# Linear attention inside a four-layer kernel: the output projection in three passes of rounded high and low parts

## The chip, the cores and the metric

The kernel runs on one core of a Trainium2 chip. The metric is the device time of one execution in microseconds, the median of three runs. TensorE multiplies matrices; VectorE (DVE), ScalarE (ACT) and GpSimd (POOL) work on tiles; SyncE (SP) and GpSimd issue transfers. Each engine runs its own instruction stream in order, and streams meet only at semaphores: a `wait_ge` stops everything behind it on its engine.

## The reference

Four layers in a row, each adding its result to `x` of shape (4, 256, 64, 64): window attention, linear attention, channel attention, dynamic convolution, each on a group norm of `x`. The change is in the second layer. Cut to what matters:

```python
ms = jnp.concatenate([qkv, agg], axis=1)          # 64 heads of 8 channels, from two scales
q, k, v = ...                                     # q and k through relu, v with a column of ones
kv = jnp.einsum('bgnd,bgne->bgde', k, v)
out = jnp.einsum('bgnd,bgde->bgne', q, kv)
out = out[..., :-1] / (out[..., -1:] + EPS)       # the division
x = x + _conv2d(out, w_proj)                      # 512 channels in, 256 out: the projection and the residual
```

## The kernel before

The whole program is a sequence of blocks: group norm, window attention, group norm, qkv projection, grouped convolution, `linear_attention`, group norm, channel attention, group norm, dynamic convolution. A block begins when the one before has ended on all engines. `linear_attention` takes 2792 to 3548 us of the profiled execution.

It works on 4 images. For each image the 512 channels are ST = 4 tiles of 128, and the 4096 pixels are NPC = 8 chunks of PC = 512. First comes the sum over keys and values (`turn` transposes a chunk of keys and of values on TensorE, ScalarE and VectorE copy them out of PSUM, `accumulate` multiplies them into `pkv`), 32 times for each image. Then, for each of NI = 32 pairs (chunk, tile) of an image, numbered i, comes one step of the main loop: `ratio` multiplies queries by the summed keys and values (numerators and denominators, 8 records in the profile), `divide` on VectorE adds EPS, takes the reciprocal and multiplies twice, `back` transposes the result on TensorE into the one buffer `att_bank`, ScalarE copies it to `att` in SBUF, and `project` multiplies it by the weights `wp` into `pp`, two matmuls of 512 columns that accumulate over the four tiles of a chunk. After the fourth tile VectorE adds `pp` to the residual `xr` (`add`), and GpSimd stores the chunk (`pool.dma_start` of `x_out`) and loads a later one into the same buffer (`load`).

The order on TensorE is written out by hand (the loop at the end of its function). In step i of image b it does: `ratio(b, i)`, `turn` and `accumulate` for image b + 1 (if there is one), `project(b, i - 1)`, `back(b, i)`. So the projection lags one step behind its own transpose. At i = 0 of a later image the order is `turn`, `accumulate`, `project(b - 1, 31)`, `ratio(b, 0)`, `back(b, 0)`. In the last image (b = 3) there is no `turn` and no `accumulate`. The first image's sum of keys and values has a loop of its own ahead of the main loop.

ScalarE's order in a step: `copy_keys`, then at eight of the 32 steps (`CLIP_AT`) `clip_queries`, which waits for queries that SyncE loads, then the copy of `att`. VectorE's: `divide`, `copy_values`, and `add` at every fourth step. GpSimd does nothing here but transfers: two loads ahead, then for each chunk a store once it is added, and a load into the same buffer, for which it waits until the store has landed. All matmuls are in float32, each of which the profile shows as two records. Buffers that matter: `att` two, `attp` two, `att_bank` one, `pp` one, `xr` two.

Of the kernel before, what the change touches and what calls it, by code (L numbers as in the profile page):

```python
# [6 lines left out]
ACT = mybir.ActivationFunctionType  # L7
AX = mybir.AxisListType
F32 = mybir.dt.float32
F32R = mybir.dt.float32r  # L10

B, C, HH, WW = 4, 256, 64, 64
NPX = HH * WW
PART = 128
HALVES = C // PART
# [966 lines left out]
ST = SCALES * HEADS1 // TG  # L982
# [3 lines left out]
def linear_attention(nc, scales, x_in, x_out, w_proj_t, head_mask, ident_in):  # L986
# [3 lines left out]
    with ctx:  # L990
        sb = lambda n, s, dt=F32: ctx.enter_context(nc.sbuf_tensor(f"d_{n}", s, dt))
        pb = lambda n, s: ctx.enter_context(nc.psum_tensor(f"d_{n}", s, F32))
        sem = lambda n: nc.alloc_semaphore(name=f"d_{n}")
        TPS = ST // SCALES
        PC = 512
        NPC = NPX // PC
        SUB = PC // PART
        SPB = SUB // 2
        NI = NPC * ST
# [6 lines left out]
        kvp = [sb(f"kvp{u}", [PART, SUB, 2 * PART + 1]) for u in range(NKV)]  # L1006
        kvm = [sb(f"kvm{u}", [PART, ST, ONE]) for u in range(2)]
        wp = sb("wp", [PART, ST, C])
        hm = sb("hm", [PART, PART])
        ident = sb("ident", [PART, PART])  # L1010
        den = [sb(f"den{u}", [PART, SUB, TG]) for u in range(2)]
        attp = [sb(f"attp{u}", [PART, SUB, PART]) for u in range(2)]
        att = [sb(f"att{u}", [PART, PC]) for u in range(2)]
        xr = [sb(f"xr{u}", [PART, HALVES, PC]) for u in range(2)]
        keys_turned = pb("keys_turned", [PART, SUB, PART])
        values_turned = pb("values_turned", [PART, SUB, PART])
# [2 lines left out]
        att_bank = pb("att_bank", [PART, PC])  # L1019
        pp = pb("pp", [PART, HALVES, PC])  # L1020
        ratios = ratio_banks[:, :, 0:SPB * ONE].rearrange("p b (s n) -> p b s n", n=ONE)
        consts_in = sem("consts_in")
        wp_in = sem("wp_in")
# [10 lines left out]
        den_steps = sem("den_steps")  # L1034
        attended = sem("attended")
        turned_back = sem("turned_back")
        att_copied = sem("att_copied")
        projected = sem("projected")
        added = sem("added")
        x_loaded = [sem(f"x_loaded{u}") for u in range(2)]  # L1040
# [2 lines left out]
        QPT = NPX // PC  # L1043
# [56 lines left out]
        @block.gpsimd  # L1100
        def _(pool):
            def of_chunk(t, b, c):
                return t[b:b + 1, :, c * PC:(c + 1) * PC].rearrange("b (h p) n -> p (b h) n", p=PART)

            def load(k):
                if k >= 2:

                    pool.wait_ge(stored[k % 2], k // 2 * 16)
                pool.dma_start(xr[k % 2][:], of_chunk(x_in, *divmod(k, NPC))).then_inc(x_loaded[k % 2], 16)

            load(0)
            load(1)
            for k in range(B * NPC):
                pool.wait_ge(added, (k + 1) * HALVES)
                pool.dma_start(of_chunk(x_out, *divmod(k, NPC)), xr[k % 2][:]).then_inc(stored[k % 2], 16)
                if k + 2 < B * NPC:
                    load(k + 2)
            for u in range(2):
                pool.wait_ge(stored[u], B * NPC // 2 * 16)

        @block.tensor
        def _(pe):
            pe.wait_ge(consts_in, 32)
            pe.wait_ge(ones_ready, NKV)

            def turn(j):

                g, k = divmod(j, QPH)
                if k == 0:
                    pe.wait_ge(kv_in[g % NH], (g // NH + 1) * (2 * len(HALF_RUNS[g % 2]) * 16))  # L1130
                if j:

                    pe.wait_ge(keys_copied, j)
                    pe.wait_ge(values_copied, j)
                for bank, buf in ((keys_turned, kt), (values_turned, vt)):
                    for e in range(SUB):
                        last = nc.tensor.transpose(bank[:, e, :], buf[g % NH][:, k * PC + e * PART:k * PC + (e + 1) * PART], ident[:])
                last.then_inc(turned, 1)

            def accumulate(j):  # L1140
                tile, k = divmod(j, QPT)
                pe.wait_ge(keys_copied, j + 1)
                pe.wait_ge(values_copied, j + 1)
                if k == 0 and tile:

                    pe.wait_ge(sums_masked, tile * 2)
                for e in range(SUB):
                    last = nc.tensor.matmul(pkv[:, 0:PART + 1], lhsT=kvp[j % NKV][:, e, 0:PART],
                                            rhs=kvp[j % NKV][:, e, PART:2 * PART + 1],
                                            start=k == 0 and e == 0, stop=k == QPT - 1 and e == SUB - 1)  # L1150
                last.then_inc(summed, 1)

            def ratio(b, i):
                c, st = divmod(i, ST)
                if c % (NPC // 2) == 0:
                    pe.wait_ge(q_positive, b * (2 * ST) + (2 * c // NPC) * ST + st + 1)
                if c == 0:
                    pe.wait_ge(sums_masked, (b * ST + st + 1) * 2)
                if b or i:

                    pe.wait_ge(attended, b * NI + i)
                for s in range(SUB):
                    queries = qt[:, st, c * PC + s * PART:c * PC + (s + 1) * PART]
                    last = nc.tensor.matmul(ratios[:, s // SPB, s % SPB, :], lhsT=queries, rhs=kvm[b % 2][:, st],
                                            start=True, stop=True)
                last.then_inc(rated, 1)

            def back(b, i):
                pe.wait_ge(attended, b * NI + i + 1)
                if b or i:  # L1170

                    pe.wait_ge(att_copied, b * NI + i)
                for s in range(SUB):
                    last = nc.tensor.transpose(att_bank[:, s * PART:(s + 1) * PART], attp[i % 2][:, s], ident[:])
                last.then_inc(turned_back, 1)

            def project(b, i):
                c, st = divmod(i, ST)
                pe.wait_ge(att_copied, b * NI + i + 1)
                if st == 0 and (b or c):  # L1180

                    pe.wait_ge(added, (b * NPC + c) * HALVES)
                for m in range(HALVES):
                    last = nc.tensor.matmul(pp[:, m, :], lhsT=wp[:, st, m * PART:(m + 1) * PART],
                                            rhs=att[i % 2][:], start=st == 0, stop=st == ST - 1)
                last.then_inc(projected, 1)

            for j in range(NQ):
                turn(j)
                if j:  # L1190
                    accumulate(j - 1)
            pe.wait_ge(wp_in, 16)
            for b in range(B):
                for i in range(NI):
                    if i or not b:
                        ratio(b, i)
                    j = (b + 1) * NQ + i
                    if b + 1 < B:
                        turn(j)
                    if b + 1 < B or i == 0:  # L1200
                        accumulate(j - 1)
                    if i:
                        project(b, i - 1)
                    elif b:
                        project(b - 1, NI - 1)
                        ratio(b, 0)
                    back(b, i)
            project(B - 1, NI - 1)

        @block.scalar  # L1210
        def _(act):
            def copy_keys(j):
                act.wait_ge(turned, j + 1)
                if j >= NKV:

                    act.wait_ge(summed, j - NKV + 1)
                nc.scalar.activation(kvp[j % NKV][:, :, 0:PART], keys_turned[:], ACT.Relu).then_inc(keys_copied, 1)

            def clip_queries(b, v, st):
                act.wait_ge(q_in[v][st // 2], (b + 1) * (2 * len(HALF_RUNS[v]) * 16))  # L1220
                part = slice(v * (NPX // 2), (v + 1) * (NPX // 2))
                nc.scalar.activation(qt[:, st, part], qt[:, st, part], ACT.Relu).then_inc(q_positive, 1)

            for j in range(NQ):
                copy_keys(j)
            for st in range(ST):
                clip_queries(0, 0, st)
            for b in range(B):
                for i in range(NI):
                    if b + 1 < B:  # L1230
                        copy_keys((b + 1) * NQ + i)
                    if i in CLIP_AT:
                        clip_queries(b, 1, CLIP_AT[i])
                    if b + 1 < B and i - NI // 2 in CLIP_AT:
                        clip_queries(b + 1, 0, CLIP_AT[i - NI // 2])
                    act.wait_ge(turned_back, b * NI + i + 1)
                    if b or i >= 2:

                        act.wait_ge(projected, b * NI + i - 1)
                    nc.scalar.activation(att[i % 2][:], att_bank[:], ACT.Copy).then_inc(att_copied, 1)  # L1240

        @block.vector
# [958 lines left out]
```

## Time and profile before

| | us |
|---|---|
| median of 3 runs | 8986.69 |
| lowest, highest | 8982.88, 8989.02 |
| the profiled execution | 8987.96 |
| its span in the trace | 8986.0 |

| engine | busy, us | share of the span |
|---|---|---|
| TensorE, matmuls | 8007.1 | 89% |
| VectorE | 5706.7 | 64% |
| GpSimd | 4530.7 | 50% |
| ScalarE | 3532.7 | 39% |

All times in the views are microseconds from the start of the span unless marked ns. A matmul row of a timeline is a run of equal instructions: its start, how long it lasts, the engine, the line, output <- inputs, shapes, and xN records; a bracket behind it is the idle time of the engine just before it and what ended it. Matmuls are pipelined, so a run's duration reaches beyond the start of the next run; the distance from start to start is what a run costs. The granted clock is TensorE's clock as a share of 2.4 GHz; 0.5 is 1.2 GHz.

### The profile page before, as it was taken

To read this page: it belongs to the slowest core of one execution; us is meant where nothing else is said; L and a number is where in the kernel's file an instruction comes from. 1 tells how busy PE (TensorE), PEld (TensorE's weight loads), DVE (VectorE), ACT (ScalarE), POOL (GpSimd) and SP (SyncE) were. 2 spreads that over 40 slices of the span, in tenths; PEclk is the share of its full clock that TensorE was granted. 3 is DMA by queue.
4 is the path that set the end of the run, shared out by engine and by line. 5 is a ranking of instruction groups with operands and counts; after the bars stand their busy time and mean duration, and the time that the engine had idled before them with its cause. 6 is when DMAs were issued, how large, how long until landed. Compare 5 with 4: busy or idle time off the path is not lost. (4 is left out here: it accounts for less than half of the span.)

```text
span 8986.0 us, 157002 instructions
## 1 busy us (share of the span) xinstructions
PE 8007.1 (89%) x55850; PEld 6800.4 (76%) x55850; DVE 5706.7 (64%) x9055; ACT 3532.7 (39%) x6841; POOL 4530.7 (50%) x2037
## 2 busy tenths in 40 slices
PE   3999995889997897499999999999999999919999
PEld 3777774679996675388888888888888888817777
DVE  4555555334442444698989889898988889841110
ACT  3545444323332332355544444454454445520000
POOL 2554543013331001288777778787877788811111
PEclk9999997999998999799999999999999999959999
DMA  5111113865555554300000000000000000071111
GB/s 208 54 56 62 53 62 150 298 191 144 147 141 171 205 200 139 131 6 18 18 18 18 13 18 6 18 18 18 18 13 18 6 18 18 8 222 61 63 62 55
DMA packets 439682, 706.22 MB, mean 79 GB/s; under 512 B 273781, under 2 KB 288629, under 8 KB 429622
## 3 DMA queue, kind: packets, MB, share of 16 engines
q1 hardware_dynamic: 400438, 521.76, 18.4%
q0 software_dynamic: 38656, 176.79, 5.3%
q8 instruction: 349, 5.72, 0.3%
q14 instruction: 239, 1.96, 0.1%
HBM read 425.22 MB, written 273.22 MB: 78 GB/s over the span
## 5 line engine op out<-in xcount | busy, mean ns | idle before, releaser
L1740 POOL TENSOR_TENSOR e_ev<-e_se,e_v 128x2048 f32<-128x2048 f32 (+1 forms) x896 | 3311.7, 3713 | 915.4 <-ACT e_se L1706 914.7
L1706 ACT ACTIVATE e_se<-e_stage 128x512 f32<-128x512 f32 x3136 | 1878.4, 599 | 2082.4 <-PE e_stage L1580 2052.2
L1830 DVE SCALAR_TENSOR_TENSOR e_stage<-e_k,e_rl,e_qp 128x512 f32<-128x512 f32 x3136 | 2308.1, 748 | 319.5 <-ACT e_se L1706 277.3
L1587 PE MATMUL e_pv_sum<-e_ident,e_ev 128*128 128x128 f32 x12544 | 1873.5, 273 | 34.9 <-issue 34.5
L1587 PE MATMUL e_pe_sum<-e_ident,e_se 128*128 128x128 f32 x12544 | 1878.8, 272 | 0.1
L1587 PEld LDWEIGHTS e_pe_sum<-e_ident,e_se 128*128 128x128 f32 x12544 | 1556.6, 140 | 227.4 <-issue 1.8
L1587 PEld LDWEIGHTS e_pv_sum<-e_ident,e_ev 128*128 128x128 f32 x12544 | 1488.1, 141 | 266.3 <-issue 212.3
L1580 PE MATMUL e_stage<-e_top,e_minus 128*128 128x512 f32 x3136 | 1510.0, 481 | 46.8 <-DVE e_stage L1830 44.9
L377 POOL TENSOR_TENSOR a_pr<-a_pr,a_rden 128x480 f32<-128x480 f32 x512 | 494.6, 987 | 672.1 <-DVE a_rden L601 672.1
L863 POOL DMA_DIRECT2D agg<-c_ot x384 | 329.1, 862 | 871.7 <-DVE c_ot L922 760.0
L1580 PEld LDWEIGHTS e_stage<-e_top,e_minus 128*128 128x128 f32 x3136 | 597.6, 191 | 96.4 <-DVE e_stage L1830 72.8
L1569 PE MATMUL e_pj<-e_xb,e_wt 128*128 128x385 f32 (+5 forms) x1280 | 570.1, 529 | 73.8 <-ACT e_v L1680 60.9
L898 PE MATMUL c_pa<-c_x_high,c_w_high 128*128 128x320 f32 x1920 | 603.1, 314 | 34.2 <-DVE c_w_low L962 34.2
L564 ACT ACTIVATE a_pr<-a_ps,a_nmax 128x240 f32<-128x240 f32 x1024 | 458.8, 459 | 419.6 <-DVE a_nmax L595 419.6
L898 PE MATMUL c_pa<-c_x_high,c_w_low 128*128 128x320 f32 x1920 | 604.8, 315 | 0.0
L898 PE MATMUL c_pa<-c_x_low,c_w_high 128*128 128x320 f32 x1920 | 603.0, 314 | 0.0
L1806 DVE SCALAR_TENSOR_TENSOR e_ext<-e_near,e_rl,e_ext 128x512 f32<-128x512 f32 x768 | 576.2, 750 | 0.9
L595 DVE TENSOR_REDUCE a_nmax<-a_ps 128x2 f32<-128x480 f32 x512 | 312.8, 653 | 338.8 <-PE a_ps L459 331.6
L1787 DVE TENSOR_REDUCE e_near<-e_pair 128x192 f32<-128x768 f32 (+2 forms) x512 | 517.5, 1011 | 0.6
L2135 DVE TENSOR_TENSOR f_xr<-f_pc,f_xr 128x512 f32<-128x512 f32 x64 | 44.2, 691 | 743.2 <-PE f_pc L2048 743.2
L2002 POOL TENSOR_TENSOR f_x_low<-f_xb,f_x_high 128x1400 fp32r<-128x1400 f32 x32 | 106.3, 3327 | 800.6 <-ACT f_x_high L2078 800.6
L2048 PE MATMUL f_pc<-f_x_high,f_w_high 128*128 128x512 f32 x1152 | 467.9, 406 | 22.3 <-POOL f_x_low L2002 22.3
(150 smaller groups left out, 12078.9 us busy)
## 6 DMA issues: line engine op xcount, KB each, us to landing
xn<-n_xnp POOLq DMA_DIRECT2D x32, 2450.0 KB, 15.0
qkv<-b_ot SPq DMA_DIRECT2D x120, 512.0 KB, 5.9
c_xt<-qkv SPq DMA_DIRECT2D x384, 160.0 KB, 3.8
agg<-c_ot POOLq DMA_DIRECT2D x384, 160.0 KB, 2.5
n_xt<-x SPq DMA_DIRECT2D x24, 2048.0 KB, 11.9
a_xb<-xn SPq DMA_DIRECT2D x32, 840.0 KB, 6.8
e_xb<-xn SPq DMA_DIRECT2D x16, 1540.0 KB, 6.9
f_xb<-xn SPq DMA_DIRECT2D x32, 700.0 KB, 6.2
```

The source lines that it names most:

```text
L377: nc.gpsimd.tensor_tensor(w, w, by, ALU.mult).then_inc(normalised, 1)
L564: last = nc.scalar.activation(pr[P % BUF][:, i, e, :], ps[:, 2 * s + i, e * NK:(e + 1) * NK], ACT.Exp, bias=nmax[P % BUF][:, i, e:e + 1], ...
L898: last = nc.tensor.matmul(pa[:, u, b, 0:NBLK * WW].rearrange("p (k c) -> p k c", c=WW), lhsT=w[u][:, dx].rearrange("p o y -> p (o y)"), rh ...
L1569: last = nc.tensor.matmul(out, lhsT=wt[:, w, g, (h % 2) * PART:(h % 2 + 1) * PART], rhs=rhs, start=g == 0, stop=g == HALVES - 1)
L1580: nc.tensor.matmul(stage[:, bank_of(t, j), :], lhsT=minus[:], rhs=top[h][:, u * TPX:(u + 1) * TPX], start=False, stop=True, skip_group_che ...
L1587: last = nc.tensor.matmul(acc[:, c * PART:(c + 1) * PART], lhsT=src[:, c * PART:(c + 1) * PART], rhs=ident[:], is_transpose=True, start=j ...
L1706: nc.scalar.activation(se[(t * K2 + o) % NSE][:, i], stage[:, bank_of(t, j), :], ACT.Exp)\
L1740: nc.gpsimd.tensor_tensor(split(ev[(t * NG2 + g) % NEV][:, 0:size]), split(se[(t * K2 + o) % NSE][:, i:i + size]), window(v[h], h, u, o, i ...
L1787: nc.vector.tensor_reduce(to, pairs, AX.XY, op).then_inc(near_step, 1)
L1806: nc.vector.scalar_tensor_tensor(rows(ext[:]), win, r[:, o:o + 1], rows(ext[:]), ALU.add, op)\
L1830: nc.vector.scalar_tensor_tensor(rows(stage[:, bank_of(t, j), :]), win, rl[:, h, o:o + 1], rows(qp[:]), ALU.add, ALU.mult).then_inc(multip ...
L2048: last = nc.tensor.matmul(pc[:, u, m].rearrange("p (r c) -> p r c", c=WW), lhsT=w[:, g, t, m * PART:(m + 1) * PART], rhs=x[:, g, dy:dy + R ...
```

## The change

The projection's operands are split. ScalarE rounds the weights `wp` to `wp_high` (float32r) once, after its ninth key copy, and GpSimd computes `wp_low = wp - wp_high`. In each step ScalarE copies `att_bank` twice, to `att_high` (rounded) and to `att`, and GpSimd computes `att_low = att - att_high`. `project` is then three accumulating passes for each half: high by high, low by high, high by low. It waits for GpSimd's subtraction instead of ScalarE's copy.

Two orders change with it. On TensorE, `back(b, i)` now stands before `project(b, i - 1)` (the order at i = 0 of a later image stays). On GpSimd, the store of chunk k - 1 comes at the last tile of chunk k, behind its split, and the load of chunk k at the second tile of chunk k.

```diff
+        wp_high = sb("wp_high", [PART, ST, C], F32R)
+        wp_low = sb("wp_low", [PART, ST, C], F32R)
...
+        att_high = [sb(f"att_high{u}", [PART, PC], F32R) for u in range(2)]
+        att_low = [sb(f"att_low{u}", [PART, PC], F32R) for u in range(2)]
...
+            def split(b, i):
+
+                j = b * NI + i
+                pool.wait_ge(att_copied, (j + 1) * 2)
+                if j >= 2:
+
+                    pool.wait_ge(projected, j - 1)
+                nc.gpsimd.tensor_tensor(att_low[j % 2][:], att[j % 2][:], att_high[j % 2][:].bitcast(F32), ALU.subtract)\
+                    .then_inc(att_split, 1)
+
+            def exchange(k):
+                pool.wait_ge(added, (k + 1) * HALVES)
+                pool.dma_start(of_chunk(x_out, *divmod(k, NPC)), xr[k % 2][:]).then_inc(stored[k % 2], 16)
+
             load(0)
             load(1)
+            flat = lambda t: t[:].rearrange("p s o -> p (s o)")
+            pool.wait_ge(wp_split, 1)
+            nc.gpsimd.tensor_tensor(flat(wp_low), flat(wp), flat(wp_high).bitcast(F32), ALU.subtract).then_inc(wp_split, 1)
             for k in range(B * NPC):
-                pool.wait_ge(added, (k + 1) * HALVES)
-                pool.dma_start(of_chunk(x_out, *divmod(k, NPC)), xr[k % 2][:]).then_inc(stored[k % 2], 16)
-                if k + 2 < B * NPC:
-                    load(k + 2)
+                for st in range(ST):
+                    split(k // NPC, k % NPC * ST + st)
+                    if st == ST - 1 and k:
+                        exchange(k - 1)
+                    if st == 1 and k >= 2:
+                        load(k)
+            exchange(B * NPC - 1)
...
-                    pe.wait_ge(att_copied, b * NI + i)
+                    pe.wait_ge(att_copied, (b * NI + i) * 2)
...
             def project(b, i):
                 c, st = divmod(i, ST)
-                pe.wait_ge(att_copied, b * NI + i + 1)
+                pe.wait_ge(att_split, b * NI + i + 1)
...
                 for m in range(HALVES):
-                    last = nc.tensor.matmul(pp[:, m, :], lhsT=wp[:, st, m * PART:(m + 1) * PART],
-                                            rhs=att[i % 2][:], start=st == 0, stop=st == ST - 1)
+                    for p, (w, a) in enumerate(((wp_high, att_high), (wp_low, att_high), (wp_high, att_low))):
+                        last = nc.tensor.matmul(pp[:, m, :], lhsT=w[:, st, m * PART:(m + 1) * PART], rhs=a[i % 2][:],
+                                                start=st == 0 and p == 0, stop=st == ST - 1 and p == 2)
...
-            pe.wait_ge(wp_in, 16)
+            pe.wait_ge(wp_split, 2)
...
-                    if i:
-                        project(b, i - 1)
-                    elif b:
+                    if i == 0 and b:
                         project(b - 1, NI - 1)
                         ratio(b, 0)
                     back(b, i)
+                    if i:
+                        project(b, i - 1)
...
             for j in range(NQ):
                 copy_keys(j)
+                if j == QPT:
+                    act.wait_ge(wp_in, 16)
+                    nc.scalar.activation(wp_high[:], wp[:], ACT.Copy).then_inc(wp_split, 1)
...
+                    nc.scalar.activation(att_high[i % 2][:], att_bank[:], ACT.Copy).then_inc(att_copied, 1)
                     nc.scalar.activation(att[i % 2][:], att_bank[:], ACT.Copy).then_inc(att_copied, 1)
```

## Rows read from the trace of the kernel before

**Rows 1.** The page, part 1: busy time, share and instructions of each engine.
```profile
PE 8007.1 (89%) x55850; PEld 6800.4 (76%) x55850; DVE 5706.7 (64%) x9055; ACT 3532.7 (39%) x6841; POOL 4530.7 (50%) x2037
```
**Rows 2.** Stretches: PE, PEld, DVE, ACT, POOL busy (instructions), granted clock, DMA share, GB/s.
```profile
2904.00:3010.00 106.00, 72.03 (x417) 57.47 (x418) 31.97 (x75) 29.62 (x34) 2.86 (x4) 0.78 0.55 209
3120.00:3230.00 110.00, 106.55 (x677) 84.09 (x677) 51.87 (x119) 36.03 (x49) 7.68 (x11) 0.97 0.59 199
3441.00:3544.00 103.00, 102.71 (x491) 63.06 (x490) 56.54 (x138) 25.36 (x35) 10.01 (x14) 1.00 0.32 104
```
**Rows 3.** Timeline of one step of the first three images, from ratio to ratio.
```profile
3202.82 1.15 PE L1164 MATMUL d_ratio_banks<-d_kvm,d_qt 128*128 128x144 f32 x8
...
3204.85 0.76 DVE L1278 TENSOR_TENSOR d_attp<-d_ratio_banks,d_den 128x256 f32<-128x256 f32 x2
...
3205.57 1.88 PE L1184 MATMUL d_pp<-d_att,d_wp 128*128 128x512 f32 x4
...
3207.29 0.60 PE L1174 MATMUL d_att_bank<-d_ident,d_attp 128*128 128x128 f32 x4
...
3207.73 1.15 PE L1164 MATMUL d_ratio_banks<-d_kvm,d_qt 128*128 128x144 f32 x8
3207.93 0.60 ACT L1240 ACTIVATE d_att<-d_att_bank 128x512 f32<-128x512 f32 x1 [2.45 <-PE d_att_bank L1174]
```
**Rows 4.** Timeline of one step of the last image, from back to back.
```profile
3483.05 0.66 PE L1174 MATMUL d_att_bank<-d_ident,d_attp 128*128 128x128 f32 x4
...
3483.54 1.15 PE L1164 MATMUL d_ratio_banks<-d_kvm,d_qt 128*128 128x144 f32 x8
...
3484.52 1.88 PE L1184 MATMUL d_pp<-d_att,d_wp 128*128 128x512 f32 x4
...
3485.57 0.76 DVE L1278 TENSOR_TENSOR d_attp<-d_ratio_banks,d_den 128x256 f32<-128x256 f32 x2
...
3486.38 0.66 PE L1174 MATMUL d_att_bank<-d_ident,d_attp 128*128 128x128 f32 x4
```
**Rows 5.** Timeline of the qkv projection: first and last of 28 passes in a row.
```profile
1749.65 0.39 PE L746 MATMUL b_pq<-b_x_high,b_w_low 128*128 128x512 f32 x1
...
1755.77 0.39 PE L746 MATMUL b_pq<-b_x_high,b_w_low 128*128 128x512 f32 x1
```
**Rows 6.** Timeline at the last change of image: ratio, then back.
```profile
3436.66 1.15 PE L1164 MATMUL d_ratio_banks<-d_kvm,d_qt 128*128 128x144 f32 x8
...
3439.71 0.66 PE L1174 MATMUL d_att_bank<-d_ident,d_attp 128*128 128x128 f32 x4 [1.91 <-DVE d_attp L1278]
```
**Rows 7.** Groups by shape, GpSimd: busy us, mean ns, idle before and its releaser.
```profile
L377 POOL TENSOR_TENSOR a_pr<-a_pr,a_rden 128x480 f32<-128x480 f32 x512 | 494.6, 987 | 672.1 <-DVE a_rden L601 672.1
...
L2002 POOL TENSOR_TENSOR f_x_low<-f_xb,f_x_high 128x1400 fp32r<-128x1400 f32 x32 | 106.3, 3327 | 800.6 <-ACT f_x_high L2078 800.6
```
**Rows 8.** Timeline at the stage's end: the last back and the last project.
```profile
3543.05 0.66 PE L1174 MATMUL d_att_bank<-d_ident,d_attp 128*128 128x128 f32 x4
...
3544.40 1.98 PE L1184 MATMUL d_pp<-d_att,d_wp 128*128 128x512 f32 x4 [0.69 <-ACT d_att L1240]
```
**Rows 9.** The tile d_wp: its DMA (duration ns, first and last start us), landing.
```profile
L1090 SPq DMA_DIRECT2D d_wp<-in_L_w_proj_t x1: 916/916/916, 2828.8 to 2828.8; - x1
...
DMA to landing us min/median/max: 15.7/15.7/15.7
```
**Rows 10.** Timeline of ScalarE: the first clips of queries.
```profile
2906.07 3.71 ACT L1222 ACTIVATE d_qt<-d_qt 128x2048 f32<-128x2048 f32 x2 [12.75 <-DMA d_qt<-qkv]
```
**Rows 11.** Waits: who waited for whom, us in total, times, longest.
```profile
POOL d_xr L1109 <- DMA x<-d_xr: 175.0, 30, 8.0
```
**Rows 12.** Waits of TensorE from 2904 to 3445 us, same columns.
```profile
PE d_pp L1184 <- ACT d_att L1240: 21.4, 3, 14.8
```
**Rows 13.** Stretches behind the second and last change of image (columns as rows 2).
```profile
3280.00:3285.00 5.00, 5.00 (x29) 4.86 (x28) 2.22 (x5) 1.20 (x2) 0.00 (x0) 0.66 0.63 194
...
3440.00:3445.00 5.00, 5.00 (x30) 3.48 (x29) 1.78 (x6) 1.19 (x2) 0.00 (x0) 1.00 0.63 195
```

More of the change, by code:

```diff
@@ L1036, in linear_attention @@
         turned_back = sem("turned_back")
+        wp_split = sem("wp_split")
         att_copied = sem("att_copied")
+        att_split = sem("att_split")
         projected = sem("projected")
```

## Prediction

> **What bounds the kernel now.** I read the page first, for the busy shares (TensorE 89% of the 8986 us [rows 1]), and then the busy time by stretch, because the page's chain of work that ended last reaches back only into the last stage (from about 8045 us) and says nothing of the stage that is changed. The linear attention runs from 2792 to 3548 us. The stretches show two different regimes in it [rows 2]: while a next image still has keys and values to sum (b = 0 to 2), TensorE is busy 106.55 of 110 us; in the last image (b = 3, from 3441 us) 102.71 of 103 us. Both look bound by TensorE. The timelines show that only the first is.
>
> In a step of the first three images [rows 3], `ratio` starts at 3202.82, `turn` and `accumulate` follow, `project` starts at 3205.57, `back` at 3207.29 and the next `ratio` at 3207.73: 4.91 us with no gap, of which `project` holds 1.72 and `back` 0.44. The divide chain of VectorE (add, reciprocal, two multiplies) ends at 3204.85 + 0.76 = 3205.61, which is 2.79 us after `ratio`; `back`, which needs it, comes 4.47 us after. So VectorE is hidden there, with 1.7 us of cover, and that cover is `project`.
>
> In a step of the last image [rows 4] there is no `turn` and no `accumulate`. `back` to `ratio` is 0.49, `ratio` to `project` 0.98, `project` to `back` 1.86: 3.33 us. `back` starts 0.05 us after the multiplies end (3485.57 + 0.76 = 3486.33) and 2.84 us after `ratio`. Without a wait `project` would have held 1.72, so the chain of VectorE already sets this step, by 0.14 us, although the busy share says 100%: `project` lies over the chain and hides nearly all of it.
>
> **The change part by part.**
>
> *Passes.* Before, the two matmuls of a step appear as four records 0.43 us apart, 1.72 us. After, there are six of one rounded pass each. The qkv projection runs the same form (128x512, contiguous, high and low parts): from 1749.65 to 1755.77 us are 27 intervals, 0.227 us each [rows 5]. Six cost 1.36 us, 0.36 less than before. The Trainium skill ("TensorE: Matmul & The Clock Gate", Back-to-back issue gap) gives N/2.4 + 2.5 ns for an isolated pass at the higher clock, 216 ns for 512 columns. By it six passes would be 1.30 us and my sum 8 us lower; the row is of the same form, so the row decides.
>
> *Order.* `back(i)` moves ahead of `project(i-1)`. This is the largest term. `back(i)` now stands directly behind `accumulate` (or, in the last image, directly behind `ratio`) and waits for the divide of its own step. Queued behind that wait are `project(i-1)`, and behind it the next `ratio`, which starts the next divide. So the step becomes a loop through VectorE: 2.84 (`ratio` to `back`) + 0.49 (`back` after a wait) + 1.36 (`project`) = 4.69 us, in all four images.
> First three images: TensorE would be ready for `back` 2.75 us after `ratio` [rows 3], so 0.09 us of the chain shows, and the step goes from 4.91 to 4.69, a gain of 0.22. I count 87 such steps (93, less six in the stretch up to 2975 us that waits for queries anyway): -19 us. Three changes of image keep their order and gain only the passes, 3 x 0.36 = -1 us.
> Last image: 3.33 becomes 4.69, since `turn` and `accumulate` are missing and the cover of `project` is gone. 31 x 1.36 = +42 us.
>
> *The residual add.* Every fourth step VectorE adds two tiles after the last projection of a chunk. Before, `back` lay between that projection and `ratio`. After, `ratio` follows directly, and the add (about 1.3 us) delays the next divide. The change of image already has this order: `ratio` at 3436.66, `back` at 3439.71, 3.05 us against 2.84 [rows 6]. So +0.21 for 20 steps in the first three images (+4 us) and 7 in the last (+1.5 us).
>
> *Splits.* ScalarE makes two copies of about 0.6 us, starting 0.64 us after `back` [rows 3]; GpSimd then subtracts 128x512. No row has that size: by 480 columns in 987 ns it is 1.05 us, by 1400 in 3327 ns 1.22 us [rows 7]; I take 1.2, the rate of the row that is also a subtraction into rounded form. The low part is ready about 0.64 + 1.2 + 1.2 = 3.1 us after `back(i)` with the semaphores; `project(i)` comes after the next `back`, 4.69 + 0.49 = 5.2 us after. Two microseconds of slack: nothing, and if the slack were gone each microsecond beyond it would cost one per step. Where ScalarE clips queries between (1.9 us, four times per half image) the slack is just used up. At the change of image `project(31)` comes 3.6 us after its `back`: still covered. At the very end it is not: `back` at 3543.05, `project` at 3544.40 [rows 8]; now about 3.15 us instead of 1.35, less 0.4 for shorter passes: +1.4 us.
>
> *Weights' split.* ScalarE waits for the projection's weights behind its ninth key copy, and all later key copies stand behind that. The weights' transfer is issued at 2828.8 and takes 15.7 us to land [rows 9], so ScalarE may stand still until about 2845 us, and `turn` with it. But the opening is paced by transfers, and the first `ratio` waits for a clip of queries that ScalarE starts at 2906.07 after 12.75 us of idle time for their DMA [rows 10]. Whatever is late by less than that is hidden. Cost 0; with the cover gone it is the stop less that idle time, 3 us.
>
> *GpSimd's transfers.* `load(k)` and `exchange(k-1)` with 0.7 us of issuing each now stand between subtractions. Before, GpSimd waited 175.0 us in 30 times, 8.0 at most, for a store to land before loading [rows 11]; now two steps (9.4 us) lie between, so it waits little and no subtraction is late. A chunk's load has three steps to land. Cost 0. The first store and reload, 1 MB, move behind the longest wait for queries (below); at the 209 GB/s of that stretch [rows 2] this is 5 us of traffic, partly on other queues: between 0 and -5, I take -3 us.
>
> *Waits for queries.* Where a clip waits for its queries, the copies of `att` stand behind it and TensorE waits: 21.4 us in 3 times, 14.8 the longest, so some 3.3 each for the other two [rows 12]. They end when a DMA lands, not when TensorE is ready. The some 6.5 steps between issue and clip give nothing for the two short ones (2 x 6.5 x 0.22 = +3), and restarting now passes through two copies and a subtraction: +0.7 each of three, +2.
>
> *The clock.* In the last image TensorE will idle 1.7 us of each 4.69. At a change of image it idles 1.91 [rows 6]; after the second of the three the granted clock of the next 5 us was 0.66, after the last 1.00 [rows 13]. 0.66 over 5 us is 3.4 us at 1.2 GHz and the rest at 2.4. Some of the 32 new gaps will be followed by such a dip. TensorE works 60% of the new step, so a dip takes 3.4 x 0.6 / 2 = 1.0 us, and a little more where it stretches the chain: 1.1. Ends: none (0) and all (+35). The rows have one dip in two; these gaps are a little shorter, and I take seven in 32, +8 us.
>
> **Sum**, against the profiled execution's 8987.96 us: first three images -19 - 1 + 4 + 3 + 2 - 3 = -14; last image 42 + 1.5 + 8 = +51.5; end +1.4. Together +39, 9027; the median is 1.3 below the profiled run: 9026 us.
>
> **The rivals.**
> (a) The clock stays low for half of the last image. For it: a gap in every step, where today there is one in 32, and one of the two shown was followed by a dip. Against: a dip ends by itself within 5 us in the rows. At 1.2 GHz `ratio` (+1.0), `back` (+0.5) and `project` (+1.3) stretch, +2.8 a step; 15 steps: +43 in place of +8, 9061 us.
> (b) GpSimd slows VectorE. Divide chain and add run beside a GpSimd subtraction for the first time here. Against it: the subtraction runs from 1.9 to 3.1 us after `back`, the divide starts at 3.04, so they hardly meet. With 0.2 us more in each of 118 looped steps: +24, 9050 us. The Trainium skill ("GPSIMD Engine Reference", Key points) says that GpSimd shares its SBUF interfaces with VectorE, with contention where VectorE has two SBUF inputs or a 2-port mode; the divide and the add each read PSUM for one operand.
> (c) The other side: the query waits go. The first three images last 536 us where 96 steps of 4.91 are 471, so 65 us are waits for queries and what follows them. If the later stores and loads let the queries land in time, these go. It ends faster once more than 39 us of the 65 go beyond what I count; with 60, 8966 us. Against: the loads moved are 1 MB in the stretch where the long waits are, worth 5 us.
> (d) The rounded passes are not one pass each, and take 0.43 us: 6 x 0.43 is 1.2 more than I count, 128 times, about 9180 us. The qkv rows speak against it.
>
> **How the numbers follow.** Forecast 0.69, (a) 0.14, (b) 0.07, (c) 0.05, (d) 0.01, and 0.04 for the gain and loss terms just cancelling. A difference of 0.2% (18 us) is about what a measurement of this kernel can tell from no change. The forecast's own spread is from 9012 (no dips, full transfer gain) to 9045. The range takes in (a), (b) and part of the cancelling: 9004 to 9062. Faster 0.04, same 0.07, slower 0.89.
>
> **What would show it.** The profile after should have `back` waiting on VectorE's multiplies in nearly every step: about 0.1 us in the first three images, 1.7 us in the last (some 50 to 60 us in total); steps of 4.69 us in both, the last image lasting about 150 us instead of 107; projection records 0.227 us apart; GpSimd's subtraction near 1.2 us with no TensorE wait behind it. I am wrong if the last image's steps stay near 3.3 us, if `project` waits for GpSimd, or if TensorE's query waits change by over 10 us.

## The result: 0.4% slower, lost in the last image

| | before | changed |
|---|---|---|
| median, us (5 runs each) | 8987.23 | 9025.25 |
| lowest to highest | 8982.88 to 8989.02 | 9022.46 to 9032.19 |
| profiled execution / its span | 8987.96 / 8986.0 | 9023.35 / 9021.4 |

The ratio is 1.0039, interval 1.0028 to 1.0050. The busy shares of the page hardly tell the two kernels apart; TensorE has less to do (8007.1 us in [rows 1]) and the time is longer:

```profile
PE 7984.4 (89%) x56106; PEld 6863.7 (76%) x56106; DVE 5703.0 (63%) x9055; ACT 3595.9 (40%) x6970; POOL 4693.3 (52%) x2166
```

A step of the first three images after the change, in the timeline (columns as in [rows 3]):

```profile
3196.97 1.14 PE L1190 MATMUL d_ratio_banks<-d_kvm,d_qt 128*128 128x144 f32 x8
...
3198.99 0.76 DVE L1309 TENSOR_TENSOR d_attp<-d_ratio_banks,d_den 128x256 f32<-128x256 f32 x2
...
3199.80 0.66 PE L1200 MATMUL d_att_bank<-d_ident,d_attp 128*128 128x128 f32 x4
3200.22 0.47 PE L1211 MATMUL d_pp<-d_att_high,d_wp_high 128*128 128x512 f32 x1
...
3201.66 1.27 POOL L1124 TENSOR_TENSOR d_att_low<-d_att,d_att_high 128x512 fp32r<-128x512 f32 x1 [3.44 <-ACT d_att L1271]
3201.68 1.14 PE L1190 MATMUL d_ratio_banks<-d_kvm,d_qt 128*128 128x144 f32 x8
```

`back` starts 0.05 us after the multiplies end (3198.99 + 0.76), 2.83 after `ratio`, and the step is 4.71 us instead of 4.91. `project` has gone behind `back` and takes 1.46 us to the next `ratio`. A step of the last image, to compare with [rows 4]:

```profile
3490.05 0.66 PE L1200 MATMUL d_att_bank<-d_ident,d_attp 128*128 128x128 f32 x4 [1.69 <-DVE d_attp L1309]
3490.47 0.47 PE L1211 MATMUL d_pp<-d_att_high,d_wp_high 128*128 128x512 f32 x1
...
3491.92 1.26 POOL L1124 TENSOR_TENSOR d_att_low<-d_att,d_att_high 128x512 fp32r<-128x512 f32 x1 [4.25 <-ACT d_att L1271]
3491.94 1.14 PE L1190 MATMUL d_ratio_banks<-d_kvm,d_qt 128*128 128x144 f32 x8
...
3493.96 0.75 DVE L1309 TENSOR_TENSOR d_attp<-d_ratio_banks,d_den 128x256 f32<-128x256 f32 x2
3494.77 0.66 PE L1200 MATMUL d_att_bank<-d_ident,d_attp 128*128 128x128 f32 x4 [1.69 <-DVE d_attp L1309]
```

The same loop, and now 1.69 us of idle TensorE in it: 4.72 us instead of 3.33. Who TensorE waited for in the whole stage (us in total, times, longest):

```profile
PE d_att_bank L1200 <- DVE d_attp L1309: 61.7, 35, 2.0
...
PE d_keys_turned L1163 <- ACT d_kvp L1244: 22.8, 2, 13.0
PE d_att_bank L1200 <- ACT d_att L1271: 17.9, 3, 12.9
...
PE d_pp L1211 <- POOL d_att_low L1124: 2.8, 5, 1.1
```

The wait for VectorE has 35 entries: the 31 steps of the last image and the four points where it stood before. GpSimd is waited for 2.8 us in all. By starts of rows, the 35.4 us between the spans lie here:

| stretch | before | changed | difference | forecast |
|---|---|---|---|---|
| span's start to first `ratio` | 2908.1 | 2910.0 | +1.9 | 0 |
| to the last change of image (`back` of [rows 6]) | 531.6 | 511.7 | -19.9 | -14 |
| to the last `back` | 103.3 | 155.7 | +52.3 | +51.5 |
| to the span's end | 5442.9 | 5444.0 | +1.1 | +1.4 |

### The profile page after: what moved, and what is told of

The parts are those of the page before. It is cut to its first block and busy times, and to the rows that moved or that the text cites. A ratio compares the mean times of both kernels' runs of the same rounds, so it can differ in the third digit from the quotient of the medians.

```text
span 9021.4 us, 157898 instructions
## 1 busy us (share of the span) xinstructions
PE 7984.4 (89%) x56106; PEld 6863.7 (76%) x56106; DVE 5703.0 (63%) x9055; ACT 3595.9 (40%) x6970; POOL 4693.3 (52%) x2166
```

## The experiments

Theory 1 is that of the prediction: the divide on VectorE closes a loop with TensorE, and the position of `project` decides whether it is covered. Theory 2 is the rival that the eye falls on, since it is what the change added: the copies and GpSimd's subtraction set the pace, or GpSimd slows VectorE. Each result is beside runs of the kernel before on the same chip.

### The old order with everything else changed

```diff
-                    if i == 0 and b:
-                        project(b - 1, NI - 1)
-                        ratio(b, 0)
-                    back(b, i)
-                    if i:
-                        project(b, i - 1)
+                    if i:
+                        project(b, i - 1)
+                    elif b:
+                        project(b - 1, NI - 1)
+                        ratio(b, 0)
+                    back(b, i)
```

> The changed kernel with TensorE's old order (project(i-1) before back(i)), all else as changed. Theory 1 (the loop through VectorE's divide sets the changed steps): the wait at back goes, but project now stands 3.2 us too near its own transpose, since two copies and the subtraction take 3.2 us after back. First three images: project is ready to start 3.2 us after back, so nearly no wait, step 4.6 us (-0.12 each). Last image: project waits for GpSimd some 1.7 us in every step, step 3.2 + 1.4 = 4.6 us, about as bad as now. Time about 9010 us. Theory 2 (the new order costs nothing, the loss in the last image is the longer chain of copies and subtraction): undoing the order changes neither regime by more than 0.1 us a step, 9015 to 9030 us, and the wait stands at project in both kernels.

Measured 9003.2 us beside 8986.1, ratio 1.0018 (1.0008 to 1.0027). Two steps of its last image, and its waits of TensorE from 3410 us on:

```profile
3462.38 0.50 PE L1211 MATMUL d_pp<-d_att_high,d_wp_high 128*128 128x512 f32 x1 [1.54 <-POOL d_att_low L1124]
...
3463.87 0.60 PE L1200 MATMUL d_att_bank<-d_ident,d_attp 128*128 128x128 f32 x4
...
3467.00 0.50 PE L1211 MATMUL d_pp<-d_att_high,d_wp_high 128*128 128x512 f32 x1 [1.55 <-POOL d_att_low L1124]
```
```profile
PE d_pp L1211 <- POOL d_att_low L1124: 51.0, 33, 2.5
```

The wait moves from `back` to `project`, and from VectorE to GpSimd; the step is 4.62 us in both regimes, as theory 1 worked out. So theory 2 is false of the changed order but true of the old one: with a lag of one step and the old order, the low part comes 1.5 us late in the last image. The new order changes one exposed chain for another that is 0.1 us longer in each step, 0.3 where an add follows, and that the clock falls in (below). Together this costs: with the old order the kernel is 17 us slower than the kernel before, with the new one 38, and the two intervals do not meet. In the traces 10.6 us of the difference lie in the last image (145.0 us from first to last `back` against 155.7) and 9.5 in the first three. So the old order alone would have saved about half of the loss, and not all of it.

### The order alone, in the kernel before

The edit above in reverse, made in the kernel before: float32 passes, no split.

> The kernel before with only TensorE's order changed (back(i) before project(i-1)); no split, no rounded passes, GpSimd as before. Theory 1: the loop of the divide is 2.84 + 0.49 + 1.72 = 5.05 us in all four images. First three images +0.14 each step and +0.2 at every add: +17 us. Last image 3.33 to 5.05 in 31 steps, +53, with the adds and clock dips +64. Time about 9067 us (+80), back waiting on VectorE 1.7 us a step in the last image. Theory 2: order alone costs nothing, 8987 us.

Measured 9057.1 us beside 8986.1, ratio 1.0074 (1.0057 to 1.0090): 71 us against 80 forecast and 0 for theory 2. Its last image:

```profile
3461.75 0.66 PE L1174 MATMUL d_att_bank<-d_ident,d_attp 128*128 128x128 f32 x4 [1.70 <-DVE d_attp L1278]
3462.25 1.88 PE L1184 MATMUL d_pp<-d_att,d_wp 128*128 128x512 f32 x4
...
3463.97 1.14 PE L1164 MATMUL d_ratio_banks<-d_kvm,d_qt 128*128 128x144 f32 x8
...
3466.80 0.66 PE L1174 MATMUL d_att_bank<-d_ident,d_attp 128*128 128x128 f32 x4 [1.70 <-DVE d_attp L1278]
```

5.05 us a step with no GpSimd work in it. The order alone makes the wait. The sum was nearly met, its parts less so. In the trace the last image is 53.0 us longer where I had 64: no dip of the clock came (I had some 9 us of them), and one step of the 31 holds no projection and stays 3.33. The first three images are 10.3 us longer where I had 17. Another 7 us lie before and behind the four images, where the change has no part.

### GpSimd's subtraction twice

```diff
+        again = sb("again", [PART, PC], F32R)
...
+                if j:
+                    pool.wait_ge(att_split, j * 2)
+                nc.gpsimd.tensor_tensor(again[:], att[j % 2][:], att_high[j % 2][:].bitcast(F32), ALU.subtract).then_inc(att_split, 1)
                 nc.gpsimd.tensor_tensor(att_low[j % 2][:], att[j % 2][:], att_high[j % 2][:].bitcast(F32), ALU.subtract)\
                     .then_inc(att_split, 1)
...
-                pe.wait_ge(att_split, b * NI + i + 1)
+                pe.wait_ge(att_split, (b * NI + i + 1) * 2)
```

> The changed kernel with GpSimd's subtraction done twice in each step (the first into a spare tile), which doubles its 1.27 us. Theory 1: the low part is then ready 4.5 us after back where it is needed 5.2 us after; nothing in a usual step. At the three changes of image and at the end it comes 1 us late each, and where clips of queries stand between, some tenths: 9028 to 9038 us. Theory 2 (GpSimd's work sets the step, or slows VectorE): +1.3 us in each of 31 to 118 steps, 9065 to 9180 us.

Measured 9041.7 us beside 8986.1 (four runs, 9030.6 to 9052.7), ratio 1.0064 (1.0048 to 1.0081); the profiled execution took about 9031. A step of its last image and TensorE's wait for GpSimd from 3427 us on:

```profile
3465.13 1.26 POOL L1127 TENSOR_TENSOR d_again<-d_att,d_att_high 128x512 fp32r<-128x512 f32 x1 [2.88 <-ACT d_att L1275]
...
3466.32 0.23 DVE L1303 TENSOR_SCALAR d_den<-d_ratio_banks 128x64 f32<-128x64 f32 x1 [3.12 <-PE d_ratio_banks L1194]
3466.36 1.26 POOL L1128 TENSOR_TENSOR d_att_low<-d_att,d_att_high 128x512 fp32r<-128x512 f32 x1
3466.58 0.55 DVE L1306 RECIPROCAL d_den<-d_den 128x64 f32<-128x64 f32 x1
3467.17 0.76 DVE L1313 TENSOR_TENSOR d_attp<-d_ratio_banks,d_den 128x256 f32<-128x256 f32 x2
...
3467.98 0.66 PE L1204 MATMUL d_att_bank<-d_ident,d_attp 128*128 128x128 f32 x4 [1.70 <-DVE d_attp L1313]
```
```profile
PE d_pp L1215 <- POOL d_att_low L1128: 4.2, 3, 2.3
```

GpSimd works 1.26 us more in each of 128 steps, 161 us, and the step stays 4.72 us. From 3466.36 to 3467.62 it even runs beside most of the divide chain, which lasts from 3466.32 to 3467.93 and whose instructions keep their 0.23, 0.55 and 0.76 us. Over the whole of the four images the mean of a reciprocal is 553 ns here and in the kernel before, of a multiply 419 and 419, of an add 687 and 686, although 110 of the 128 reciprocals and 50 of the 64 adds lie at least nine tenths inside a subtraction here. That settles the rival in which GpSimd slows the divide and the add.

One instruction of VectorE outside this chain is held up by GpSimd: the second of the two that mask the sums of keys and values once for each tile (`d_kvm`, 128x16), 0.23 us long when alone.

```profile
3427.98 1.26 POOL L1128 TENSOR_TENSOR d_att_low<-d_att,d_att_high 128x512 fp32r<-128x512 f32 x1
3428.08 1.19 DVE L1297 TENSOR_SCALAR d_kvm<-d_hm,d_pkv 128x16 f32<-128x16 f32 x1
```

It ends at 3429.27, 0.03 us after the subtraction. It began inside a subtraction nine times in all the traces (three here, two each with the old order, the lag of two and ratio ahead), lasted 0.31 to 1.19 us, and each time ended 0.03 us after it; the three times that the subtraction began after it, it kept its 0.23. In the changed kernel it never met one. It runs four times an image, so it costs little here.

In the median it costs some 18 us more than the change (against 3 to 13 expected), in the trace 7.5; the waits for GpSimd grow from 2.8 to 11.7 us in 11 places. The profiled execution was the fastest of the four; where the others lost their time is not known.

### The residual's add narrowed in the last image

```diff
+                px = slice(0, 16 if b == B - 1 and c < NPC - 1 else PC)
                 for m in range(HALVES):
-                    nc.vector.tensor_tensor(xr[k % 2][:, m, :], pp[:, m, :], xr[k % 2][:, m, :], ALU.add).then_inc(added, 1)
+                    nc.vector.tensor_tensor(xr[k % 2][:, m, px], pp[:, m, px], xr[k % 2][:, m, px], ALU.add).then_inc(added, 1)
```

> The changed kernel with the residual's add in the last image cut from 512 to 16 columns for all but its last chunk (the rest of the residual's sum is left out there), so that every idle gap of TensorE in the last image is 1.69 us and none 1.91. Theory 1 with a clock that falls only after the longer gaps: no dip of the granted clock in the last image, whose first to last back shrinks from 155.7 to about 145 us; 9014 us. Rival (any gap of this size can be followed by a dip, the adds are chance): still some six dips, 9023 us.

Measured 9011.5 us beside 8986.1, ratio 1.0028 (1.0018 to 1.0037); expected 9014. In the changed kernel the granted clock falls behind the longer gap at 3483.88 (stretches, columns as [rows 2]; the last three numbers are the granted clock, DMA share, GB/s):

```profile
3480.00:3485.00 5.00, 3.09 (x20) 2.62 (x19) 2.73 (x6) 1.16 (x3) 1.26 (x1) 1.00 0.01 4
3485.00:3490.00 5.00, 3.36 (x13) 2.68 (x11) 1.53 (x4) 0.66 (x2) 1.94 (x2) 0.66 0.30 82
3490.00:3495.00 5.00, 3.25 (x20) 2.78 (x21) 1.53 (x4) 1.09 (x2) 1.26 (x1) 1.00 0.06 23
```

Such a step takes 6.2 to 6.3 us instead of 4.72. In the changed kernel 6 of the 7 gaps of 1.91 us inside the last image are followed by one, and none of the 24 of 1.69. The three other kernels with the same last image show the same: 6, 5 and 4 of 7 (weights later, store early, subtraction twice), and none of 24 each time. With the narrow add all gaps inside the image are 1.69 or 1.70, and from the third step on every step is 4.71 to 4.73. The forecast of no dip still failed in one place, behind the gap of 1.91 at the change of image itself, which the edit leaves as it is:

```profile
3430.00:3435.00 5.00, 3.06 (x17) 2.71 (x17) 1.72 (x5) 1.08 (x2) 1.25 (x1) 0.61 0.52 176
3435.00:3440.00 5.00, 3.95 (x16) 3.16 (x14) 0.94 (x3) 1.09 (x2) 1.94 (x2) 0.70 0.59 169
3440.00:3577.00 137.00, 87.68 (x522) 73.99 (x522) 46.42 (x131) 38.67 (x62) 46.04 (x43) 1.00 0.21 70
```

The first two steps take 3.92 and 6.48 us there, and the last image 147 instead of the 145 that I expected; in the changed kernel that gap was followed by no dip. So a longer gap is followed by a dip often, not always, and no dip began behind a shorter one. But the gap alone isn't the cause: the kernel with the order alone has the same seven gaps of 1.91 and no dip:

```profile
3490.00:3495.00 5.00, 3.30 (x18) 2.13 (x17) 1.85 (x5) 0.60 (x1) 0.00 (x0) 1.00 0.00 0
3495.00:3500.00 5.00, 3.09 (x17) 1.92 (x16) 2.42 (x6) 0.60 (x1) 1.00 (x2) 1.00 0.29 108
3500.00:3505.00 5.00, 3.30 (x18) 2.13 (x17) 1.53 (x4) 1.72 (x2) 0.43 (x1) 1.00 0.35 105
```

There the gap stands among float32 passes and a longer `project`, and the longer gaps come every 20.4 us instead of 19.1 (20.7 with a dip between). Which of these keeps the clock up was not tried.

### The weights' rounding later

```diff
                 copy_keys(j)
-                if j == QPT:
-                    act.wait_ge(wp_in, 16)
-                    nc.scalar.activation(wp_high[:], wp[:], ACT.Copy).then_inc(wp_split, 1)
+            act.wait_ge(wp_in, 16)
+            nc.scalar.activation(wp_high[:], wp[:], ACT.Copy).then_inc(wp_split, 1)
```

> The changed kernel with ScalarE's rounding of the weights (and its wait for their transfer) moved from behind the ninth key copy to behind the last one of the opening. If ScalarE's stop of some 10 us there is not hidden, the first ratio goes back from 2910 to 2908 us and the time falls by 2 us to 9023. If the opening is paced by transfers alone, the first ratio stays within its scatter and the time at 9025 us.

Measured 9015.8 us (9011.1 to 9030.3) beside 8982.1, ratio 1.0038 (1.0024 to 1.0051), the change's own ratio. TensorE's waits in the opening, first in the changed kernel, then here:

```profile
PE d_keys_turned L1163 <- ACT d_kvp L1244: 9.9, 1, 9.9
PE d_keys_turned L1163 <- DMA d_vt<-agg: 2.2, 1, 2.2
```
```profile
PE d_keys_turned L1163 <- DMA d_vt<-agg: 9.1, 4, 4.7
```

ScalarE's stop costs TensorE 9.9 us, and waits for keys and values of about that length disappear in exchange (10.7 us in the kernel before). From the first `turn` to the first `ratio` it is 97.4 us in the kernel before, 99.2 in the changed one and 102.1 here, without the stop. The other traces with the stop have 97.7 to 100.2. So the +1.9 us is within the scatter of the opening, and no cost of the stop shows in it.

### Store and load as early as before

```diff
-                    if st == ST - 1 and k:
+                    if st == 0 and k:
                         exchange(k - 1)
-                    if st == 1 and k >= 2:
-                        load(k)
+                    if st == ST - 1 and k and k + 1 < B * NPC:
+                        load(k + 1)
```

> The changed kernel with GpSimd's store of chunk k-1 moved from the last tile of chunk k to its first, and the load of chunk k+1 to its last tile (before: load of chunk k at its second tile): two to three steps earlier each, as the kernel before had them. If the later place of the transfers is what shortened TensorE's waits for queries (14.8 to 12.9 us at 2972 us, 3.45 to 1.55 at 3216), the waits grow back and the time by 2 to 4 us, 9028 us. If not, 9025 us.

Measured 9023.4 us (9011.0 to 9035.0) beside 8982.1, ratio 1.0047 (1.0033 to 1.0061). TensorE's waits for `att` are 18.9 us in two places, against 17.9 in three. The difference from the change is inside both intervals: my -3 us for the later transfers is neither shown nor excluded.

### A lag of two steps

`project(i - 2)` before `back(i)`, and VectorE's `add` one step later; passes and splits as changed.

```diff
-                    if i == 0 and b:
-                        project(b - 1, NI - 1)
-                        ratio(b, 0)
-                    back(b, i)
-                    if i:
-                        project(b, i - 1)
+                    if i == 0 and b:
+                        project(b - 1, NI - 2)
+                        ratio(b, 0)
+                    elif i == 1 and b:
+                        project(b - 1, NI - 1)
+                    elif i >= 2:
+                        project(b, i - 2)
+                    back(b, i)
+            project(B - 1, NI - 2)
             project(B - 1, NI - 1)
```

> The changed kernel with the projection lagging two steps and standing before back: ratio(i), turn, accumulate, project(i-2), back(i); VectorE's add one step later. Three rounded passes as changed. Theory 1: project again covers the divide, and the copies and subtraction have more than a step. First three images 0.99 + 0.87 + 0.89 + 1.36 + 0.44 = 4.55 us a step, bound by TensorE; last image 2.84 + 0.49 = 3.33 us, the kernel before's. Against the kernel before -0.36 in some 90 steps: 8957 us. Theory 2 (copies and subtraction set the last image's step): it stays at 4.7 us, 9005 us or more.

Measured 8944.0 us beside 8982.1, ratio 0.9960 (0.9946 to 0.9973), 13 us less than expected. A step of its last image:

```profile
3463.58 0.66 PE L1200 MATMUL d_att_bank<-d_ident,d_attp 128*128 128x128 f32 x4 [0.30 <-DVE d_attp L1312]
3464.07 1.15 PE L1190 MATMUL d_ratio_banks<-d_kvm,d_qt 128*128 128x144 f32 x8
...
3464.96 0.49 PE L1211 MATMUL d_pp<-d_att_high,d_wp_high 128*128 128x512 f32 x1
...
3466.11 0.76 DVE L1312 TENSOR_TENSOR d_attp<-d_ratio_banks,d_den 128x256 f32<-128x256 f32 x2
3466.92 0.66 PE L1200 MATMUL d_att_bank<-d_ident,d_attp 128*128 128x128 f32 x4 [0.30 <-DVE d_attp L1312]
```

3.33 us again, with the same copies, the same subtraction and the same passes as the change: only the place of `project` differs, and that of the add. In the first three images the step is 4.58 us instead of 4.91, so nearly all of the gain of the passes (0.36) is there. The 13 us that I did not expect lie there too: in the trace these images take 487.2 us against 531.6, 44 less where I had 32, and the last image is as long as before. The waits for queries are 17.9 us instead of 21.4, and TensorE stands at the lower clock for 30 us instead of 56; how the 12 us divide between these was not tried.

### Ratio ahead in the last image

As in the version with a lag of two, and in the last image `ratio(i + 1)` goes into the two banks that `turn` no longer uses, so that two ratios are under way.

```diff
+        ratio_views = [t[:, :, 0:SPB * ONE].rearrange("p b (s n) -> p b s n", n=ONE) for t in (ratio_banks, turned_banks)]
...
+                if b == B - 1 and i:
+                    pe.wait_ge(attended, b * NI + i - 1)
+                    if i == 1:
+                        pe.wait_ge(keys_copied, B * NQ)
+                        pe.wait_ge(values_copied, B * NQ)
...
+                    if b == B - 1 and i + 1 < NI:
+                        if i:
+                            ratio(b, i + 1)
```

> As the kernel with a lag of two, and in the last image, where the banks of turn are free, ratio(i+1) goes into them while ratio(i) is being divided (two sets of banks in turn). Theory 1: the last image's loop through VectorE is cut, its step becomes 0.99 + 1.36 + 0.44 = 2.8 us, bound by TensorE: -0.53 in 31 steps, 8940 us. If VectorE's add and divide together (2.0 us a step) or ScalarE's copies set it, between 2.8 and 3.3 us a step: 8940 to 8957 us.

Measured 8929.1 us beside 8982.1, ratio 0.9941 (0.9927 to 0.9954): the fastest version here. It is 11 us below what I expected, since the lag of two had gained 13 more than its forecast. A step of its last image:

```profile
3460.45 0.60 PE L1210 MATMUL d_att_bank<-d_ident,d_attp 128*128 128x128 f32 x4
...
3460.88 1.15 PE L1200 MATMUL d_ratio_banks<-d_kvm,d_qt 128*128 128x144 f32 x8
...
3461.77 0.49 PE L1221 MATMUL d_pp<-d_att_high,d_wp_high 128*128 128x512 f32 x1
...
3463.26 0.60 PE L1210 MATMUL d_att_bank<-d_ident,d_attp 128*128 128x128 f32 x4
```

2.81 us, and 3.1 where an add stands between. The loop is cut, and TensorE is the bound.

### Ratio ahead alone

The same second set of banks in the kernel before, with its float32 passes and lag of one.

> The kernel before (float32 passes, no split, its own order with a lag of one), changed only in the last image: ratio(i+1) goes into the free banks of turn while ratio(i) is being divided. Theory 1: the last image's step, set by VectorE at 3.33 us, becomes TensorE's own 0.99 + 1.72 + 0.44 = 3.15 us: -0.18 in 31 steps, 6 us faster, about 8976 us beside 8982. Then of the 53 us that the kernel with a lag of two and ratio ahead gains, nearly all rests on the rounded passes once they are covered. If instead the second set of banks is what brings that gain, it is 20 us or more here too.

Measured 8984.3 us beside 8985.1, ratio 0.9998 (0.9989 to 1.0007). In the trace the last image's step is 3.13 us, 3.43 at the adds, instead of 3.33, so 4 us are gained there and the median doesn't resolve them. The second set of banks is worth little with float32 passes, where TensorE's own work is 3.14 us a step; behind the lag of two and with rounded passes it is worth 14.3 (the last image lasts 89.0 us instead of 103.3). The 53 us of the version above thus rest on the rounded passes, once they are covered. A lag of two with float32 passes was not run: by the steps it has nothing to gain, since TensorE holds 4.91 us in the first three images and the chain 3.33 in the last.

## Why the prediction was right, point by point

The median is 9025.25 us where 9026 was forecast. By its steps:

*Passes.* Forecast 0.227 us each and 1.36 for six. Within the group that holds, but the first pass after `back` takes 0.31 to 0.35, so `project` lasts 1.46 from its start to the next `ratio`, while `back` gives up 0.07 (0.42 instead of 0.49). Together 1.88 against 1.85, which is the 4.72 against 4.69 of the step.

*Order.* This step carried the forecast, and held. The chain from `ratio` to `back` stayed 2.83 in both regimes. Last image: +42 forecast; 30 steps at +1.39 are +41.7 (the step from i = 0 to 1 holds no projection and stays 3.33). The experiments show the cause: the order alone makes the wait, and a lag of two, with everything that the change added still there, removes it. What they show besides, and the prediction did not ask, is that the old order with the rest of the change would also have lost, by GpSimd's low part.

*Add.* +0.21 forecast, 4.93 against 4.72 measured.

*Splits.* 1.2 us forecast for the subtraction, 1.27 measured, and hidden in all usual steps. The doubled subtraction confirms the 2 us of slack. The last projection waits for GpSimd, as counted (3.17 us after its `back` instead of 1.35). `project` waiting for GpSimd was named as a sign of being wrong; it does so in four other places, 1.7 us in all: three behind waits for queries, where 2 us were counted and 1.4 came, and one at the last change of image, 0.24 us, where the prediction said covered.

*The clock.* Right in sum, wrong inside. I took seven dips of 1.1 us, spread over all 32 gaps by chance; there are six of 1.6, all behind the longer gaps. The term that was mis-sized is the dip. The rule that TensorE works 60% of the step does not hold inside it: the lower clock falls on `back` and `project`, which run without a gap (`project` takes 2.71 us instead of 1.47), so nearly all of 3.4 / 2 counts, and `ratio` and the next divide start that much later. That 7 x 1.1 is near 6 x 1.6 is luck. The rival with a low clock for half of the image did not come; the granted clock over the last image is 0.93.

*First three images.* Forecast -14, measured -19.9 in one execution. The third image has no wait for queries and shows -5.9 between its changes where the same terms give -5.7, but 1.65 us of it are a dip behind the second change ([rows 13]) that the changed kernel did not have. Without it the steps gained 4.2: each is 4.72 instead of the forecast 4.69, and the change of image with the step behind it gains 0.06 instead of 0.58. So the terms of the steps were too hopeful by 1.5 us an image. Two others were too gloomy. The waits for queries and their restarts were put at +5, less 3 for the later transfers; the waits went from 21.4 to 17.9 us, with 1.4 us for restarts. And the clock had no term in these images: TensorE stood at the lower clock for 46 us instead of 56, worth up to 5 us. Two other kernels with the same first three images (narrow add, weights later) need 2.8 and 6.8 us longer for them than this execution, so the miss is no larger than the scatter, and part of the -19.9 may be just that.

*Weights.* Cost 0 forecast. No cost shows. The cover that I named (ScalarE's idle time before the first clip) was hardly used, 11.42 us are left of 12.75; the stop was taken up earlier, by the waits for keys and values.

## What to carry to other kernels

When an instruction is moved ahead on an engine that runs in order, ask what was lying over the wait that it now meets, and ask it in every regime of the loop: here the last image lacks the work that covers the wait in the others, and a busy share of 100% hid that it was already 0.14 us into the chain. If a step needs more time between producing and using, lag it by one more step before moving it across its own producer; that kept the cover and gained what the shorter passes were worth. Banks that fall idle in the last round of a pipeline can hold a second item under way.

## What the runs showed of the hardware that was not expected

Inside the last image the granted clock fell after 6 of 7 gaps of 1.91 us and after none of 24 gaps of 1.69 us, in steps that are otherwise alike (21 of 28 and none of 96 in the four traces with such an image); the same 1.91 us among float32 passes was followed by no fall. A fall made the step of 4.72 us last 6.3.

A GpSimd subtraction of 1.26 us that ran beside VectorE's divide chain lengthened none of its instructions. The Trainium skill ("GPSIMD Engine Reference", Key points) warns of contention for the interfaces that GpSimd shares with VectorE, where VectorE has two SBUF inputs or is in a 2-port mode. By it the multiplies and the add, each with one operand in PSUM, are not among those that suffer, and the traces agree (419 and 687 ns with the subtraction twice, 419 and 686 without any). The small mask instruction, which reads one tile in SBUF and a column in PSUM, did suffer: begun inside a subtraction, it ended 0.03 us after it in nine of nine cases, up to 1.19 us long instead of 0.23. The reciprocal, whose one tile is in SBUF too, did not (553 ns). Why one waits and the other does not, no run here shows.
